# A new order of work for the attention of a sandwich layer, and its last chunk's rest at steps 24 and 25

## The chip, the cores and the metric

The kernel runs on one core of a Trainium2 chip. The metric is the device time of one launch in microseconds (us). The engines are TensorE (PE; its weight loads are shown apart as PEld), VectorE (DVE), ScalarE (ACT), GpSimd (POOL) and SyncE (SP), which here issues most of the DMAs. PE's clock has two levels, 1.2 and 2.4 GHz; a granted clock of 1.00 in the profile is the upper one.

## The reference

Input x is 4 x 2048 x 256 in float32. Biases, all of them drawn with a spread of 0.1, are left out of this sketch.

```
n   = layernorm(x)
q,k,v = n@wq, n@wk, n@wv                      # 16 heads of 16
s   = q @ k.T / 4, causal                     # 2048 x 2048 for each of 64 (batch, head) pairs
x   = x + layernorm(softmax(s) @ v @ wo)
n   = layernorm(x)
e   = the two best of 8 experts, by token 0 of each batch entry (n[:,0] @ Wr)
x   = x + layernorm(mean over both of gelu(n@W1[e]) @ W2[e])
```

## The kernel before

**Stage a** (to about 206 us) normalises x in 16 chunks of 512 tokens, multiplies out q, k and v and writes them to DRAM. q and k are written as three bf16 parts whose sum is the float32 value: ACT casts the high part (L1122), POOL subtracts it, ACT casts the middle part (`middle`, L972, 128 x 2048), DVE subtracts that for the low part (`low`, L976), and SP stores all three. For the last of the 16 chunks the middle, the low part and the store do not fit in stage a: they are handed to stage b as `rest_of_a`.

**Stage b** (about 206 to 1690 us) is the attention. It takes four heads at a time: `it` 0 to 7 and `g` 0 or 1 give 16 such groups. A group's 2048 queries are four chunks `c` of 512, and chunk c has 4(c+1) key tiles of 128. One (group, chunk, key tile) is a **key step** `j`; there are 640, 80 for each `it`, 40 for each group. A key step costs:

- scores, PE L1382: for each of four heads two products (64 rows of the array, then 33 rows), up to 512 columns, into the four banks of `b_psS`. Heads 0 and 2 use the lower 64 rows of the array (half 0), heads 1 and 3 the upper 64 rows (half 1).
- two exponentials, ACT L1339, each of two heads (128 x 1024 at full width), into `b_prob`, which holds four steps
- on the diagonal a causal mask on POOL, L1309
- values, PE L1399: four products of 128 rows x 32 columns of the array with float32 operands, all heads side by side, into `b_psO`. The trace shows 8 matmuls for one key step.
- at the end of a chunk a copy of `b_psO` (ACT L1349) and its store.

The exponent needs each row's greatest score beforehand, to subtract it. So PE computes the scores of a later chunk once more, roughly, into `b_ring` (L618, with L616 for the causal part of a diagonal block), and DVE takes their maximum from there (L628). The ring has three banks. There are 2336 such maximum jobs, each in one half of the array; 54 of them are done in stage a. When all jobs of a chunk are done, DVE reduces once more and transposes (L634, L644), SP stores the result and loads it again as a row of `g_qT` (L651, L655), and only then can the chunk's scores start.

DVE has three more duties in stage b. Once for each `it` from 1 on, at its step 20, it takes the reciprocals of the row sums of the `it` before (L236, `INVERT_AT`). Once, it takes the `low` of the last chunk of stage a. And at the end it runs `front`, the output projection and first layer norms of the first batch entry, which PE mixes with the last key steps.

**What sets the order.** PE, DVE, ACT and SP each walk the same list, `ORDER`, which `read_orders` makes of the strings in `ORDERS`. Each sign is one piece of work:

```
"0" "1"   the next score product of half 0 or 1 (4 of each half per key step)
"a" "b"   the next maximum job of half 0 or 1
"v"       the value product of the next key step
"p" "q" "r" "y" "l"   pieces of front: projection, two square roots, transposes, expert scores
```

The engines run each other's work free only through semaphores: a maximum job waits until DVE has emptied the bank three jobs back; the first score product of a pair of heads waits for the exponential of the same pair one key step back; a value product waits for both exponentials of its step. The strings were drawn up by a program outside the kernel; no cost model is in the kernel.

Where the rest is placed is read in the same walk. In ACT's loop, with `last` true for the last of the score products that an exponential waits for:

```
if last:
    exponentials(j, s)
if last and (j, s) == (REST_MIDDLE_AT, 1):
    rest_of_a.scalar(act)          # the cast, L972
```

and in DVE's loop `if last and (j, s) == (REST_LOW_AT, 1): rest_of_a.vector(v)` (L976, which first waits for the cast), and for the reciprocals `if last and s == 1 and at == INVERT_AT and it > 0: chunks.invert_sums(v, it - 1)`.

**Stage c** (from 1690 us) multiplies out the experts and the rest of the projections, chunk by chunk. It is the same code before and after.

## Time and profile before

| | |
|---|---|
| median of 3 runs | 1991.49 us |
| lowest, highest | 1989.31, 1994.93 us |
| the profiled execution's own time | 1991.74 us |
| its span in the trace | 1990.0 us |
| instructions | 39435 |

The profile counts an engine as busy while an instruction is in it. Two matmuls in the two halves of the array overlap, and the share counts their union, so a PE that is busy 98% of the time may still have one half idle. "Idle before" is the time in which an engine did nothing ahead of the instruction named, with the engine that ended the wait. In the timeline, instructions of one kind that follow each other stand in one row, with their count behind an x.

### The profile page before, as it was taken

The numbers are of one execution on the slowest core, as the hardware profiler recorded it, in microseconds if no ns is written. First come the engines' busy times: TensorE is split into PE (matmuls) and PEld (weight loads), VectorE is DVE, ScalarE is ACT, GpSimd is POOL, SyncE is SP. The second block draws the span as 40 slices with busy tenths as digits, with TensorE's granted clock in tenths as the row PEclk, the third lists the DMA queues.
The fourth block names the chain that finished last, engine by engine and source line by source line (L and its number), as shares of the span: only waits on it lengthen the run. The fifth ranks groups of instructions, "written<-read, shape, count | busy, mean of one in ns | idle before, by whom it ended". The sixth has DMA issues, their size and how long they took to land. (4 is left out here: it accounts for less than half of the span.)

```text
span 1990.0 us, 39435 instructions
## 1 busy us (share of the span) xinstructions
PE 1950.9 (98%) x15684; PEld 854.6 (43%) x15684; DVE 1784.6 (90%) x3574; ACT 1365.3 (69%) x1655; POOL 295.6 (15%) x358
## 2 busy tenths in 40 slices
PE   9999999999999999999999999999999998999998
PEld 6655333333333333333333333333333343667665
DVE  7876999999999999999999999999999985799984
ACT  5766757777777777777777777777777767333432
POOL 4333101011111111010111111110101211322100
PEclk9999999999999999999999999999999999999999
DMA  6877606040404124250504041232506213344321
GB/s 180 255 220 209 136 11 123 16 93 9 92 23 85 44 55 68 35 88 11 93 9 92 16 91 42 58 61 42 92 7 136 82 38 119 85 127 124 96 69 43
DMA packets 151706, 162.93 MB, mean 82 GB/s; under 512 B 58466, under 2 KB 124386, under 8 KB 151522
## 3 DMA queue, kind: packets, MB, share of 16 engines
q1 hardware_dynamic: 146658, 151.98, 32.7%
q0 software_dynamic: 4864, 8.44, 1.9%
q8 instruction: 123, 2.02, 0.4%
q14 instruction: 61, 0.50, 0.1%
HBM read 100.03 MB, written 60.29 MB: 81 GB/s over the span
## 5 line engine op out<-in xcount | busy, mean ns | idle before, releaser
L628 DVE TENSOR_REDUCE b_pmax<-b_ring 128x1 f32<-128x512 f32 (+4 forms) x2282 | 1329.0, 647 | 62.3 <-PE b_ring L618 51.1
L1339 ACT ACTIVATE b_prob<-b_psS 128x1024 f32<-128x1024 f32 (+3 forms) x1280 | 1084.8, 895 | 359.3 <-PE b_psS L1382 353.9
L1382 PE MATMUL b_psS<-g_qT,g_kT 33*128 33x512 bf16 (+7 forms) x5120 | 832.8, 348 | 9.8 <-ACT b_prob L1339 7.7
L618 PE MATMUL b_ring<-g_kT,g_qT 64*128 64x512 bf16 (+3 forms) x2498 | 712.1, 348 | 3.9 <-DVE b_pmax L628 2.1
L1399 PE MATMUL b_psO<-b_prob,g_v 128*32 128x512 f32 (+3 forms) x5120 | 595.5, 540 | 0.4 <-ACT b_outT L1349 0.3
L1382 PEld LDWEIGHTS b_psS<-g_qT,g_kT 64*128 64x128 bf16 (+1 forms) x5120 | 295.6, 94 | 462.7 <-ACT b_prob L1339 349.4
L1309 POOL TENSOR_SCALAR_AFFINE_SELECT b_prob<-b_prob 128x512 f32<-128x512 f32 x256 | 163.4, 638 | 1296.6 <-ACT b_prob L1339 1296.3
L618 PEld LDWEIGHTS b_ring<-g_kT,g_qT 64*128 64x128 bf16 x2498 | 220.5, 94 | 251.4 <-DVE b_pmax L628 177.7
L616 PE MATMUL b_ring<-later,query_of 64*128 64x128 bf16 x988 | 190.6, 219 | 2.0 <-DVE b_pmax L628 1.5
L1399 PEld LDWEIGHTS b_psO<-b_prob,g_v 128*32 128x32 f32 x5120 | 103.2, 108 | 168.0 <-issue 133.5
L1753 PE MATMUL c_psH<-c_yT,c_w1e 128*128 128x512 f32 x256 | 116.7, 604 | 10.4 <-ACT c_hT L1674 7.5
L1166 PE MATMUL a_psQK<-c_cc,a_w 128*128 128x512 f32 x256 | 115.8, 599 | 1.2 <-ACT c_cc L1086 1.2
L1766 PE MATMUL c_psO<-c_w2e,c_hT 128*128 128x256 f32 x512 | 113.4, 380 | 0.0
L616 PEld LDWEIGHTS b_ring<-later,query_of 64*128 64x128 bf16 x988 | 87.6, 94 | 54.9 <-DVE b_pmax L628 26.9
L1766 PEld LDWEIGHTS c_psO<-c_w2e,c_hT 128*128 128x128 f32 x512 | 97.0, 190 | 18.7 <-issue 6.2
L1674 ACT ACTIVATE c_hT<-c_psH,c_b1e 128x512 f32<-128x512 f32 x64 | 43.1, 686 | 53.8 <-PE c_psH L1753 53.7
L1753 PEld LDWEIGHTS c_psH<-c_yT,c_w1e 128*128 128x128 f32 x256 | 47.9, 192 | 69.8 <-issue 52.3
L1166 PEld LDWEIGHTS a_psQK<-c_cc,a_w 128*128 128x128 f32 x256 | 47.2, 190 | 54.6 <-issue 53.8
L1180 PE MATMUL a_psV<-a_w,c_cc 128*128 128x256 f32 x256 | 58.8, 383 | 0.0
L99 ACT ACTIVATE c_ln_x_std<-c_ln_x_var,eps 128x4 f32<-128x4 f32 x12 | 3.6, 297 | 76.1 <-DVE c_ln_x_var L95 76.1
L628 DVE TENSOR_REDUCE b_pmax<-a_ring 128x1 f32<-128x512 f32 (+4 forms) x54 | 31.1, 617 | 26.3 <-PE a_ring L618 26.2
L976 DVE TENSOR_TENSOR a_parts<-c_inv,a_parts 128x2048 bf16<-128x2048 f32 x16 | 36.7, 2292 | 19.8 <-ACT a_parts L972 19.8
(162 smaller groups left out, 1055.9 us busy)
## 6 DMA issues: line engine op xcount, KB each, us to landing
qk_parts<-a_parts SPq DMA_DIRECT2D x64, 384.0 KB, 4.5
g_qT<-qk_parts SPq DMA_DIRECT2D x184, 128.0 KB, 4.5
g_kT<-qk_parts SPq DMA_DIRECT2D x184, 128.0 KB, 5.0
out_sums<-b_outT SPq DMA_DIRECT2D x64, 256.0 KB, 2.9
v_ones<-a_v SPq DMA_DIRECT2D x16, 544.0 KB, 5.8
g_v<-v_ones SPq DMA_DIRECT2D x32, 272.0 KB, 4.9
a_x<-in_L_attn_x SPq DMA_DIRECT2D x16, 512.0 KB, 4.9
c_x<-in_L_attn_x SPq DMA_DIRECT2D x15, 512.0 KB, 5.0
```

The lines of the kernel that those rows point to most:

```text
L616: self.nc.tensor.matmul(to[:, w - P:w], consts.query_of[half:half + HALF, :], consts.later[half:half + HALF, :], start=True, stop=False, s ...
L618: ins_ = self.nc.tensor.matmul(to, groups.qT[own, g, h // 2, 0, t * P:(t + 1) * P], groups.kT[own, g, h // 2, 0, pc * CH:pc * CH + w], sta ...
L628: self.nc.vector.tensor_reduce(pmax[:, c % 2].rearrange("p (h t) n -> p h t n", t=TT)[:, heads[0]:heads[-1] + 1:2, qt, pc], bank[:, 0:k * ...
L1166: ins_ = nc.tensor.matmul(psQK[:, i % 2], w[:, t, k, m * P:(m + 1) * P], xT[:, n % 2, k], start=(k == 0), stop=(k == KD - 1))
L1180: ins_ = nc.tensor.matmul(psV[:, t], xT[:, n % 2, k, t * P:(t + 1) * P], w[:, 2, k], start=(k == 0), stop=(k == KD - 1))
L1309: nc.gpsimd.affine_select(out=tile, in_=tile, compare_op=ALU.is_ge, fill=0.0, base=0, pattern=[[0, HG], [1, P]], channel_multiplier=-1).th ...
L1339: nc.scalar.activation(prob[:, j % PBUF, 2 * s:2 * s + 2, off:CH], psS[:, 2 * s:2 * s + 2, off:CH], ACT.Exp).then_inc(exp_done, 1)
L1382: ins_ = nc.tensor.matmul(psS[:, 2 * s + p, off:CH], kT[own, g, s, ab, kt * P:(kt + 1) * P], qT[own, g, s, ab, c * CH + off:(c + 1) * CH], ...
L1399: ins_ = nc.tensor.matmul(psO[h * VW:(h + 1) * VW, off:CH], vS[:, g, kt, h * VC:h * VC + VW], prob[:, j % PBUF, h, off:CH], start=(kt == 0 ...
L1674: nc.scalar.activation(hT[:, e, m], psH[:, i % 2], ACT.Gelu, bias=experts[b % 2].b1[:, e, m:m + 1]).then_inc(gelu_done, 1)
L1753: ins_ = nc.tensor.matmul(psH[:, i % 2], experts[b % 2].w1[:, e, k, m * P:(m + 1) * P], yT[:, k, c], start=(k == 0), stop=(k == KD - 1))
L1766: ins_ = nc.tensor.matmul(psO[:, t], hT[:, e, m, t * P:(t + 1) * P], experts[b % 2].w2[:, e, m], start=(i == 0), stop=(i == 2 * KD - 1))
```

## The change

Three things change, all in numbers and strings.

```diff
-REST_MIDDLE_AT = 26
-REST_LOW_AT = 30
+REST_MIDDLE_AT = 24
+REST_LOW_AT = 25
 REST_STORED_AT = 34
...
 ORDERS = (
-    "a101a1010b0ab1010aa0101b1010av1a110bb0001v01ab010101b0101bv0b011a101aav0b0b011bbvb0101a1010bav1a1aa1010b"
+    "a1010b0a1b01a1010a0101ab0vab010101a1v0101b0101bb01010101avba1010bv0b011a101ab0vb0101aa1010bvb0101a1010ba"
...
```

The strings are new from the first sign to the last. They hold the same signs: 2560 each of "0" and "1", 1141 each of "a" and "b", 640 "v", 15 of the front. The program that draws them up now counts three more things: the reciprocals on DVE, the rest of the last chunk on ACT and DVE, and ScalarE's idle time. Nothing is computed otherwise.

**The rest.** On ACT, in stage b of the kernel before; the names are those of the rows above (`b_prob` exponentials, `b_outT` the copy out):

```order
L1339 ACTIVATE b_prob<-b_psS 128x2x128 x2
L1349 COPY b_outT<-b_psO 128x512
L1339 ACTIVATE b_prob<-b_psS 128x1024 x6
L972 CAST a_parts<-c_inv 128x4x512
L1339 ACTIVATE b_prob<-b_psS 128x1024 x20
```

The same place after the change:

```order
L1339 ACTIVATE b_prob<-b_psS 128x2x128 x2
L1349 COPY b_outT<-b_psO 128x512
L1339 ACTIVATE b_prob<-b_psS 128x1024 x2
L972 CAST a_parts<-c_inv 128x4x512
L1339 ACTIVATE b_prob<-b_psS 128x1024 x24
```

The cast moves ahead of four exponentials: it now follows the first pair of this chunk instead of the third. On DVE, around `low`, before:

```order
L628 TENSOR_REDUCE b_pmax<-b_ring 128x1 x5
L628 TENSOR_REDUCE b_pmax<-b_ring 128x2
L628 TENSOR_REDUCE b_pmax<-b_ring 128x1 x13
L976 TENSOR_TENSOR a_parts<-c_inv,a_parts 128x4x512
L628 TENSOR_REDUCE b_pmax<-b_ring 128x1 x2
```

and after:

```order
L634 TENSOR_REDUCE b_nmax<-b_pmax 128x16
L644 STREAM_TRANSPOSE b_nmT<-b_nmax 128x32
L628 TENSOR_REDUCE b_pmax<-b_ring 128x1 x3
L628 TENSOR_REDUCE b_pmax<-b_ring 128x2
L628 TENSOR_REDUCE b_pmax<-b_ring 128x1
L628 TENSOR_REDUCE b_pmax<-b_ring 128x2
L628 TENSOR_REDUCE b_pmax<-b_ring 128x1
L976 TENSOR_TENSOR a_parts<-c_inv,a_parts 128x4x512
L628 TENSOR_REDUCE b_pmax<-b_ring 128x1
```

`low` now comes seven reductions of jobs after the end of a chunk (L634, L644: group 1's first chunk) instead of far behind it. In the strings, the signs that follow the point of `low` are `10b0bv1ab01010b01a` before and `b0101a0101v101010b` after.

**A reciprocal.** On DVE, around the first of the seven reciprocals of stage b (the one at key step 100), before:

```order
L634 TENSOR_REDUCE b_nmax<-b_pmax 128x16
L644 STREAM_TRANSPOSE b_nmT<-b_nmax 128x32
L236 RECIPROCAL b_pair_sums<-b_pair_sums 128x128
L628 TENSOR_REDUCE b_pmax<-b_ring 128x2
L628 TENSOR_REDUCE b_pmax<-b_ring 128x1 x6
```

and after:

```order
L644 STREAM_TRANSPOSE b_nmT<-b_nmax 128x32
L628 TENSOR_REDUCE b_pmax<-b_ring 128x2
L628 TENSOR_REDUCE b_pmax<-b_ring 128x1 x3
L628 TENSOR_REDUCE b_pmax<-b_ring 128x2
L628 TENSOR_REDUCE b_pmax<-b_ring 128x1 x2
L236 RECIPROCAL b_pair_sums<-b_pair_sums 128x128
L628 TENSOR_REDUCE b_pmax<-b_ring 128x1 x5
```

The reciprocal no longer follows a chunk's end directly. What PE does between the jobs changes more than DVE's own order: the signs behind the reciprocal's point are `bbb1010v1aab001010ba1` before and `vba10101a100v1a110b0a` after, so three maximum jobs come at once before, and a value product, two jobs and five score products after.

**An ordinary stretch.** On PE, from one value product (L1399) to the next, behind the value product of key step 414, before:

```order
L1399 MATMUL b_psO<-b_prob,g_v 32x512 x4
L1382 MATMUL b_psS<-g_qT,g_kT 128x512
L618 MATMUL b_ring<-g_kT,g_qT 128x512 x2
L1382 MATMUL b_psS<-g_qT,g_kT 128x512 x7
L618 MATMUL b_ring<-g_kT,g_qT 128x512
L616 MATMUL b_ring<-later,query_of 128x128
L618 MATMUL b_ring<-g_kT,g_qT 128x512
```

and after:

```order
L1399 MATMUL b_psO<-b_prob,g_v 32x512 x4
L618 MATMUL b_ring<-g_kT,g_qT 128x512
L1382 MATMUL b_psS<-g_qT,g_kT 128x512 x4
L618 MATMUL b_ring<-g_kT,g_qT 128x512 x2
L1382 MATMUL b_psS<-g_qT,g_kT 128x512 x4
L618 MATMUL b_ring<-g_kT,g_qT 128x512
```

Both hold eight score products and four maximum jobs. After the change the two halves take turns, one maximum job of each half ahead of four score products and again behind them (the form `b0101ab0101a`); 27 stretches of the new order read exactly so, and 7 of the old.

## Rows read from the trace of the kernel before

**Rows 1.** The page's first part: span, busy time of each engine.
```profile
span 1990.0 us, 39435 instructions
PE 1950.9 (98%) x15684; PEld 854.6 (43%) x15684; DVE 1784.6 (90%) x3574; ACT 1365.3 (69%) x1655; POOL 295.6 (15%) x358
```

**Rows 2.** Busy time by stretch: stretch, length, then per engine; granted clock, DMA share, GB/s.
```profile
206.00:262.00 56.00, 55.41 (x496) 19.28 (x494) 55.79 (x98) 39.47 (x48) 7.84 (x12) 1.00 0.47 84
262.00:300.00 38.00, 34.07 (x280) 12.46 (x276) 34.17 (x63) 22.79 (x25) 1.24 (x2) 0.91 0.08 27
300.00:1630.00 1330.00, 1323.15 (x12618) 485.96 (x12613) 1267.57 (x2255) 1015.54 (x1231) 159.04 (x240) 1.00 0.30 59
1630.00:1690.00 60.00, 56.10 (x436) 22.61 (x428) 34.48 (x116) 42.34 (x52) 6.04 (x8) 1.00 0.35 115
```

**Rows 3.** PE's timeline, 801 to 808: start, length, instruction, count.
```profile
803.68 1.06 PE L1399 MATMUL b_psO<-b_prob,g_v 128*32 128x512 f32 x8
804.67 0.39 PE L1382 MATMUL b_psS<-g_qT,g_kT 64*128 64x512 bf16 x1
804.68 0.39 PE L618 MATMUL b_ring<-g_kT,g_qT 64*128 64x512 bf16 x1
804.90 0.60 PE L1382 MATMUL b_psS<-g_qT,g_kT 33*128 33x512 bf16 x3
805.12 0.38 PE L618 MATMUL b_ring<-g_kT,g_qT 64*128 64x512 bf16 x1
806.17 1.06 PE L1399 MATMUL b_psO<-b_prob,g_v 128*32 128x512 f32 x8
```

**Rows 4.** PE's timeline, two value products in one, and a stretch at 969 us.
```profile
1263.36 1.92 PE L1399 MATMUL b_psO<-b_prob,g_v 128*32 128x512 f32 x16
1265.21 0.61 PE L1382 MATMUL b_psS<-g_qT,g_kT 64*128 64x512 bf16 x4
...
969.48 1.06 PE L1399 MATMUL b_psO<-b_prob,g_v 128*32 128x512 f32 x8
971.97 0.64 PE L1399 MATMUL b_psO<-b_prob,g_v 128*32 128x512 f32 x4
```

**Rows 5.** Timeline at the first reciprocal: DVE, PE, and PE's weight loads.
```profile
449.55 0.91 DVE L236 RECIPROCAL b_pair_sums<-b_pair_sums 128x128 f32<-128x128 f32 x1
...
449.96 1.06 PE L1399 MATMUL b_psO<-b_prob,g_v 128*32 128x512 f32 x8
453.02 1.06 PE L1399 MATMUL b_psO<-b_prob,g_v 128*32 128x512 f32 x8
...
451.98 0.09 PEld L616 LDWEIGHTS b_ring<-later,query_of 64*128 64x128 bf16 x1 [0.28 <-DVE b_pmax L628]
```

**Rows 6.** Timeline, 261 to 295: DVE, ACT and PE around the rest.
```profile
261.88 0.22 DVE L634 TENSOR_REDUCE b_nmax<-b_pmax 128x16 bf16<-128x64 f32 x1
...
277.84 1.89 ACT L972 CAST a_parts<-c_inv 128x2048 bf16<-128x2048 f32 x1
...
289.91 2.28 DVE L976 TENSOR_TENSOR a_parts<-c_inv,a_parts 128x2048 bf16<-128x2048 f32 x1
...
268.30 0.60 PE L1382 MATMUL b_psS<-g_qT,g_kT 64*128 64x512 bf16 x1
280.71 0.39 PE L1382 MATMUL b_psS<-g_qT,g_kT 64*128 64x512 bf16 x2 [1.34 <-ACT b_prob L1339]
292.86 0.39 PE L618 MATMUL b_ring<-g_kT,g_qT 64*128 64x512 bf16 x1 [1.63 <-DVE b_pmax L628]
```

**Rows 7.** Granted clock in a stretch of its own, as Rows 2.
```profile
268.30:275.10 6.80, 6.78 (x37) 2.89 (x39) 5.52 (x11) 3.98 (x5) 0.00 (x0) 0.52 0.07 23
```

**Rows 8.** PE's timeline in the front, 1630 to 1680.
```profile
1630.47 3.72 PE L792 MATMUL b_ring<-wo,c_cc 128*128 128x256 f32 x16
...
1678.64 0.61 PE L1382 MATMUL b_psS<-g_qT,g_kT 64*128 64x512 bf16 x4 [0.68 <-ACT b_prob L1339]
```

**Rows 9.** DVE's timeline, six reductions in a row.
```profile
352.50 3.83 DVE L628 TENSOR_REDUCE b_pmax<-b_ring 128x1 f32<-128x512 f32 x6
```

**Rows 10.** DMA queue of SP, and DVE, at the end of a chunk, 1358 to 1361.
```profile
1358.94 0.57 SPq L651 DMA_DIRECT2D shifts<-b_nmT  x1
1360.91 1.17 SPq L655 DMA_DIRECT2D g_qT<-shifts  x2
...
1358.44 0.22 DVE L634 TENSOR_REDUCE b_nmax<-b_pmax 128x16 bf16<-128x64 f32 x1
```

More of the change, by code:

```diff
@@ new lines @@
+    "10b0101abva110b0a1vb0010101abva110110b00av01010b101a10b01av101ab0va1a0101010abva1010b0101abvb010101a10ba"
+    "va10101a10b0bvb01010b01a1ava1010b0101abvb0101a1010bavab01a101a1v0b1a10ba00ab0va11010b0a1v0b0001111bb0101"
+    "010b1ava1010ba0101a1010av1a100b1a10b0v0b101aa1010bv0b0101a101abv0b1a101a10b0va1010ba1010bva1010b011a0bva"
+    "1010ba1010bva1010ba1010bv0b0b011a101abvb0101a1010bava1010b0101abvba10101a1vb00b001a1v10100b011bb01010b01"
+    "1ava110b0b0101v0ba101v",
+    "0ba1010101va11100010bb0101avb0101ab0101avvb0101ab0101av0b1a10b010ba1va1010b0101abva110b0a1vb0010101abvb0"
@@ new lines @@
+    "01a1010ba1010bvvb0101a10b01av0b011a101a0bva1010b0101abva1010b0101abvb0101a1010bav1a100ba1010bv10101aa1a0"
+    "b0a100b1ab0101abv0b01a11010bava11010b001v0101ba1010a1010101ab0v1a100b10b01ava1010bb010a1v1a100bb0101ava1"
+    "010ba1010bvb0101a101a0bva1010b0101abvb0101ab0v1a10b01a10bva1010ba1010bbvb0101a101a0bva1010b0101abvb0101a"
+    "1010bavb0101a1010bav0b0101ab0va11010ba1v1010ba1010v0b011a1010bava110b0v",
+    "101ab01010bv0101010ba1v1010b0101ab0101av01a10bv1a100b01a10bva1010ba1010bva1010b0101abva1010b0b011avb0010"
@@ new lines @@
+    "010b0101b0101a1010bva1010bv0b1a1010a1b0v1a100bb010a1vb0101a1010bavb0101a1010bavb0101a10b01av0b01010bv1aa"
+    "1a101a0bvbab010101a10bv0b011ab010a1va110b00101v1010ba1010b1010100ba1va1010ba1010aa1010av1a10b0101a0bva10"
+    "1010ba10bv0b1a101a10b0vb0101ab0101ava1010b011a0bva1010b01a10bva1010b0101abv0b0b011a10a1bvb0101ab0101ava1"
+    "010b01a10bvb0101ab0va110101ab0va110101abv0b00101abv0b0011011ab0101av0b01a1v",
+    "0b01a10101bv1010ba1010vb00011101ab0101bvb0101b010b1avb0101aa1010bvb0101ab0101avb0101a10b01ava1100b0101ab"
@@ new lines @@
+    "a11v10101a100a1010bavva1010b01b0a1va1010b0101abvb0101a10b01ava1010b0101abvb0101a1010bava1010b0101aav0b1a"
+    "010b1aab01a1010bv0b011a1a10b0v1a10b010b01vb0010a1110vab01010101a01a10aa1010bv1a1001a10b0v1a1a0b01010bava"
+    "1010b0101abv0b1a10101ab0va1010b010ba1va1010b0101bavb0101a1010bava1010b0101abvb0101ab0101ava1010b0101abva"
+    "1010b01a10bvb0101ab0va1101ab010vab0101a11v0b0a11b00v1010b0101a10b01av0101abv",
+    "010ba10101bv10101ab010v0101a1010b0101bava1010a10ab01va01010b101abva1010b01a10bvb0101a10b01ava110b0a1vb00"
@@ new lines @@
+    "a11v0101a1010ba1010bvva1010b01a10bva1010b0101abvb0101a10b01ava10101ab010bva1010b0b01a1va10101a1a00av0b1a"
+    "1a010b1ab0bv0b011a0b01a1v0b01a10101avb0010101b1bb10100101b1010a1010bav1ab010010ba1v0b01a1v0b1a1010b01av0"
+    "ba10b01011av1a0b01a1010bv1a10b010a1b0vb0101a1a100bvb0101a1010bavb0101a10b01ava10101a10b0bvb0101a10b01avb"
+    "0101ab0101ava1010ba1vb001a110b0vb00101ab0v1a1b00a11v10101a100b0101abv0101abv",
+    "1a10b01010av01010b0a11v0101a1010b0b011av101a0bvb0101ab0101avb0101ab0101avb0101ab0101ava1010b01a10bvb0010"
@@ new lines @@
+    "0v10101ab010b0101avvb0101a1010bavb0101a10b01av0b011a1a100bva1010ba1010bvb0101ab0101avb0101a1010bav1aa101"
+    "a10b0b0v010b1ab100b1bb0101bb0011avb0010101a1av01010b011bb01010b01a1va1010b0b011ava1010ba1010bvb0101a101a"
+    "b0vb0101ab0101av1a0b010b01a1va1010b0101abvb0101a1010abv0b01a101a10bvb0101ab0101ava1010b010ba1vb0101a1010"
+    "bavb0101a1010bavab0101a1vb0010b0a11vb001001a11v1010b0101a0b01a1va110b0a1010v0b0a11v",
+    "010b001a11bv0b0011011ab0101va1010ba1010bv1a10b0v1a10b0a1010bva1010b101ab0va1010b0101aava110101ab00vb0010"
@@ new lines @@
+    "1010ba1010bvvb01a10b0101avb0101a10b01ava10101a10b0bvb01010b01a1ava1010b01a10bvb0101a101ab0vab0101a0b101a"
+    "bv1a100bb0101abv0ba1101010bava110b00101va11010100aa0101a1010bvb0101abva1010b0101bav1a1a1010a0b0avb0101a1"
+    "0b01av0b01a10b01a1vb0101a1010bav0b011a0b01a1vba10101010bavb0101a1010bav0ba1010b01a1vb0101a10b01avb0101a1"
+    "00ba1vb01010abva110b001a1vb00101ab011v0b0a111100a01010b01a1vb001a1v",
+    "0b011a1010bva1b001a1100v10100ba101010b1avvb0101a1010bavb0101ab0101avb0101a0b01a1vb0101a1010bavb001a1b010"
```

122 lines of the change are left out of this document (43 added, 79 removed).

## The prediction

> **What bounds the kernel now.** I read the page's first part, then the busy time by stretch, then the timeline. The reader is to see first that PE is busy 98% of a span of 1990.0 us [rows 1], and in the body of the attention, 300 to 1630 us, 1323.15 of 1330 us; DVE stands at 1267.57 there, ACT at 1015.54 [rows 2]. PE is the bound, but its busy share hides an idle half of the array. So the length has to be read between value products, which need the whole array.
>
> An ordinary stretch: value products start at 803.68 and 806.17, 2.49 us apart. The next product starts 0.99 us after the first; products in the two halves start together (804.67 and 804.68), and each half takes a new 512-column product about every 0.22 us, 512 columns at 2.4 GHz [rows 3]. This stretch has 3072 columns in each half, 1.28 us, so a full-width value product costs 1.21 us. Two value products with nothing between take 1.92 us as a row and the next score product comes 1.85 us after the first: 0.88 + 0.97 [rows 4]. So each passage from half-array products to a value product and back costs 0.32 us.
>
> I walked the old order with two rules from these rows: a product starts when its half is free and not before the one ahead of it; value products cost as above, shorter ones in proportion to their columns. A check where the halves are balanced (2560 columns each) but two jobs of one half follow each other: columns alone give 2.28 us, the walk 2.49, and the products stand at 969.48 and 971.97, 2.49 apart [rows 4]. From the first value product to the last of the 640 the walk gives 1443.8 us, the trace 1479.6. The rest, 35.8 us, I place so:
> - front's projections and transposes on PE, not in the walk: four blocks of 3.55 us (3.72 with the overlapping tail [rows 8]) and two of 0.8 for transposes, 15.8 us. They stay.
> - the first 40 stretches: 9.8 us. DVE is busy 55.79 of 56 us up to 262 and is the bound there [rows 2]; group 0 needs all maxima of its last chunk before key step 24. They are done at 261.88 and the scores start at 268.30 only [rows 6], then run at a granted clock of 0.52, the lower level, to 275.1 [rows 7]. The cast holds PE 1.34 us, `low` 1.63 us [rows 6].
> - the seven reciprocals, 4.5 us in the eight stretches around each. At the first, value products stand 3.06 us apart, where columns give 2.28 (2560 in each half), and PE waits for DVE with 0.28 us at 451.98 [rows 5].
> - waits for ACT in the tail, such as 0.68 us at 1678.64 [rows 8]: 4.5 us. The rest, 1.2 us, is scattered.
>
> **The change part by part.** It adds and removes no instruction; everything is order.
>
> Columns. In each stretch between value products the fuller half counts. Summed over all stretches that is 1,808,896 columns before and 1,798,400 after: 10,496 fewer at 2400 per us, **-4.4 us**. Where one half gets two products in a row, the other waits: the walk's surplus over the fuller half falls from 10.6 to 5.8 us, **-4.8 us** (stretches that lose over 0.08 us in this way: 49, now 26). Value products that follow another directly fall from 23 to 13: ten more passages at 0.32 us, **+3.2 us**. Together -6.0 us. This term rests on counts, and the walk met the quiet middle (stretches 41 to 600) within 5.1 us of 1275, of which 4.5 are the reciprocals; I give it 1 us either way. No wait hides it: PE is the engine at work.
>
> A rule of the Trainium skill bears on the +3.2: "TensorEngine Tiling (Array Packing)", Key Properties, says that changing the tiling mode drains the engine. The rows agree in kind, with 0.32 us for a passage there and back; the page gives no size. It is the part of this change that goes the wrong way.
>
> Reciprocals. Each takes 0.91 us on DVE [rows 5]. A reduction of 512 columns takes about 0.62 us in a row of six (3.83 us [rows 9]), and four in 2.49 us is near DVE's limit, so a reciprocal sets the ring back by more than one bank. In the old order the fourth job behind the reciprocal's point comes 2.0 to 2.3 us later in six of seven cases (columns and value products counted), in the new one 3.3 to 3.9 us in five of seven. DVE needs 0.91 + 0.62 for the first bank. I take **-3.3 us** of the 4.5; bounds 0 (PE's surplus of work there was bought with a wait elsewhere) and -4.5.
>
> The rest. The cast (1.89 us) now comes between the exponentials of step 24 and those of 25, `low` (2.28 us [rows 6]) one step later. Behind ACT's cast, which no longer has an idle stretch ahead of it, stand the exponentials of step 25 and the ones of 26; PE waits there for the bank of step 26, about 3.1 us of its own work later, against 1.89 + 0.92 + the score's own way: a wait of 0 to 1 us where it was 1.34. Behind `low`, DVE may wait for the cast up to 1.5 us, and with `low` is away 3.8 us; the fourth job behind it comes after 4.7 us in the new order, 2.2 us in the old, so the 1.63 us go. But DVE's summed work is ahead of PE's by more: at the stretch of `low` the summed reductions less PE's walk stand at 7.9 us after and 7.1 before, which takes up to 0.8 us back. The queue of SP is not touched: the store stays at step 34. I take **-1.5 us** for the first 40 stretches beside the columns; bounds -6 (all waits and the slow clock gone) and +2.5.
>
> The clock. For 6.8 us PE ran at the lower level, behind 6.3 us in which it waited for DVE again and again [rows 6, 7]. The new order is just as dense in maxima there (16 jobs between the end of the last chunk's maxima and step 24's first score, 15 before), so I expect the fall to stay. It is half of 6.8, 3.4 us, that hangs on it. "TensorE: Matmul & The Clock Gate", Terms, prices it alike, throttled time times the missing share of pulses; by that page's rule a fall avoided gives 3.4 us more and a second fall takes as much.
>
> The tail. From the first projection on, the walk is equal (40.1 us each). The new order puts 4, not 8, score products behind the second projection and eight between the transposes where none stood: **-0.4 us**; bounds -3 and +2.
>
> The sum: -6.0 - 3.3 - 1.5 - 0.4 = -11.2 us, from the profiled execution's 1991.74 us 1980.5 us. The profiled execution lies 0.25 us above the median of the runs; I leave that in the rounding and predict **1980.5 us**.
>
> **The rivals.**
> - The gain is the column term and more: the clock does not fall, and all waits at the reciprocals and the rest go. -6.0 - 4.5 - 6 - 2 = -18.5: about 1973 us. For it: one job fewer stands ahead of step 24's first score (108, from 109), and PE's walk to it is 1 us shorter. Against: DVE is the bound in that place in both orders.
> - It is taken back: no change. The columns saved lie where PE had to wait for a bank of the ring or of the scores anyway, so a fuller half costs nothing there. For it: in the body ACT and DVE both leave PE little room, and the stretches that lose most by the walk are often those around a chunk's end, dense in jobs. Half of -9.2 and half of the reciprocals gone, +3.2 kept: 1988 to 1990 us. Against: the old walk meets the body without such waits; a stretch of 2560 columns with two jobs in one half lasts exactly as walked [rows 4].
> - DVE falls behind, which makes it slower. With four full-width jobs a stretch lasts 2.49 us by PE [rows 3], and DVE needs 4 x 0.62 = 2.48 [rows 9]. There are 222 such stretches between the 41st and the 600th in the new order (234 in the old, where they last 2.50 on the mean). If a regular order takes from DVE the pauses in which it caught up, and each is paced by DVE at 2.60, that is +22 us, less 11: about 2003 us. It decides from 0.08 us per stretch on: 222 x 0.08 = 17 us is what turns -11 into +6. Against: DVE idles 62 us of the body's 1330 [rows 2], and the old order had runs of 12 such stretches, the new one of 10 at most.
> - The maxima arrive late. From the last reduction of a chunk (1358.44) to the first load of the shifts' row 2.47 us pass [rows 10]; with the second load and a landing as long as the store's 1.97 us it is 5.6 us, and DVE may run three banks, 1.9 us, behind. The walk's distance from a last chunk's last job to its first score is 7.4 us at the least in both orders (the first group apart). At 8.5 us for the way one or two groups would wait 1 us: +1, inside the range.
>
> **How the numbers follow.** Forecast (1976 to 1985) 0.58; the larger gain 0.13; taken back, 1986 to 1991, 0.19; DVE behind, slower, 0.08; late maxima 0.02. From no change a measurement of this kernel tells about 0.3%, 6 us. The forecast and the larger gain lie beyond it but for the forecast's upper edge: faster 0.72, within 0.3% 0.20, slower 0.08. The range runs from the larger gain to the edge of no change, 1973 to 1989.5 us.
>
> **What would show it.** In the changed profile: 640 value products whose first and last lie some 1468 us apart, not 1479.6; stage c unchanged at about 300 us; DVE's busy time unchanged and its idle time smaller by about 10 us; no wait of PE for DVE at `low`; the cast's wait under 1.1 us; at the reciprocals stretches within 0.3 us of their columns. It is wrong if the first 40 stretches take over 109 us (106.6 before), if stretches with four full-width jobs last over 2.55 us, or if a chunk's first score products stand behind an idle PE.

## The result and the profile after

| | before | after |
|---|---|---|
| median | 1991.38 us (4 runs) | 1978.20 us (4 runs) |
| lowest, highest | 1989.31, 1994.93 us | 1973.95, 1982.12 us |
| the profiled execution's own time | 1991.74 us | 1982.12 us |

The ratio of the runs is 0.9932, with a 95% interval from 0.9906 to 0.9957: the change makes the kernel about 13 us faster. The forecast was 1980.5 us. It is close, but two of its steps were wrong in opposite directions, as the rest of this text shows.

The page's first part of the changed kernel, which answers to [rows 1]:

```profile
span 1980.4 us, 39435 instructions
PE 1940.9 (98%) x15684; PEld 852.9 (43%) x15684; DVE 1782.0 (90%) x3574; ACT 1363.6 (69%) x1655; POOL 294.7 (15%) x358
```

DVE is busy 2.6 us less and ACT 1.7 us less, PE 10 us less in a span 9.6 us shorter. The shares tell nothing: the gain has to be read from stretch to stretch, as before.

The busy time by stretch of the changed kernel, in the order of [rows 2]: PE, PEld, DVE, ACT, POOL, granted clock, DMA share, GB/s.

```profile
206.00:262.00 56.00, 55.28 (x488) 19.59 (x488) 55.60 (x95) 39.23 (x48) 8.77 (x12) 1.00 0.44 86
262.00:300.00 38.00, 36.98 (x319) 13.94 (x317) 36.10 (x68) 26.03 (x28) 0.63 (x1) 0.96 0.20 62
300.00:1528.00 1228.00, 1225.31 (x11811) 452.15 (x11807) 1184.87 (x2115) 945.98 (x1150) 140.83 (x222) 1.00 0.31 59
1528.00:1545.00 17.00, 10.51 (x78) 4.17 (x79) 7.34 (x14) 5.90 (x9) 1.27 (x2) 0.60 0.53 145
1545.00:1620.00 75.00, 74.55 (x695) 26.09 (x691) 71.86 (x125) 58.79 (x71) 16.92 (x16) 1.00 0.09 29
1620.00:1680.00 60.00, 56.00 (x428) 22.55 (x420) 33.92 (x116) 42.60 (x52) 4.90 (x8) 1.00 0.35 115
```

Up to 262 us little has changed: PE is busy 55.28 us and DVE 55.60, where they were 55.41 and 55.79. From 262 to 300 PE is busy 36.98 us where it was 34.07. From 300 to 1528 us PE is busy 99.8% of the time. Then comes one hole: in the 17 us from 1528 on it works 10.51 us, and its clock is granted at 0.60 there.

By value products, counted as in the prediction (a stretch runs from one value product's start to the next one's; all times from the two timelines):

| stretches | before, us | after, us | change |
|---|---|---|---|
| 1 to 40 | 106.58 | 101.72 | -4.9 |
| 41 to 600, but 582 to 584 | 1268.55 | 1253.29 | -15.3 |
| 582 to 584 | 6.48 | 16.76 | +10.3 |
| 601 to 639 | 97.96 | 98.51 | +0.6 |
| first to last value product | 1479.6 | 1470.3 | -9.3 |

From the last value product to the end, which is stage c, it takes 300.1 us, 300.2 before. So the new order saves some 20 us in two places and loses 10.3 us in one.

**The loss.** SP's queue in the changed kernel at that place (start, length, instruction). L249 and L250 are the loads of contexts and inverse sums for `front`; L651 and L655 store a chunk's maxima and load them again as a row of `g_qT`, here for the last chunk of the next to last group, whose scores begin with key step 584.

```profile
1511.10 0.64 SPq L249 DMA_DIRECT2D c_cc<-out_sums  x1
...
1521.07 2.10 SPq L250 DMA_DIRECT2D c_inv<-inverse_sums  x1
1523.21 1.00 SPq L651 DMA_DIRECT2D shifts<-b_nmT  x1
1533.25 1.20 SPq L655 DMA_DIRECT2D g_qT<-shifts  x2
```

The timeline of DVE and PE at the same place, changed kernel:

```profile
1520.95 0.22 DVE L634 TENSOR_REDUCE b_nmax<-b_pmax 128x16 bf16<-128x64 f32 x1
...
1528.97 0.38 PE L618 MATMUL b_ring<-g_kT,g_qT 64*128 64x512 bf16 x1
1535.84 1.03 PE L1382 MATMUL b_psS<-g_qT,g_kT 64*128 64x512 bf16 x4 [6.49 <-DMA g_qT<-shifts]
...
1537.33 1.02 DVE L628 TENSOR_REDUCE b_pmax<-b_ring 128x2 f32<-128x256 f32 x2 [7.25 <-PE b_ring L618]
```

DVE's last reduction for the maxima starts at 1520.95. The store L651 is issued at 1523.21, behind twelve loads of front, and the load L655, which waits for the store's landing, 10.0 us later. PE stands still for 6.49 us. Within this wait its clock falls to the lower of its two levels, and it stays there from 1531.2 to 1544.8 us, for 9.0 us of which PE works. From 1530 to 1545 us the granted clock is 0.54.

```profile
1530.00:1545.00 15.00, 9.16 (x62) 3.84 (x66) 5.41 (x10) 4.66 (x6) 0.35 (x1) 0.54 0.53 137
```

In the kernel before, DVE's last reduction started at 1539.16, the store followed 0.5 us later, and store and load stood 3.3 us apart:

```profile
1539.66 0.56 SPq L651 DMA_DIRECT2D shifts<-b_nmT  x1
1542.98 1.20 SPq L655 DMA_DIRECT2D g_qT<-shifts  x2
```

**The rest.** DVE, ACT and PE of the changed kernel around the cast and `low`, which answer to [rows 6]:

```profile
262.14 0.22 DVE L634 TENSOR_REDUCE b_nmax<-b_pmax 128x16 bf16<-128x64 f32 x1
...
272.10 1.89 ACT L972 CAST a_parts<-c_inv 128x2048 bf16<-128x2048 f32 x1
...
275.88 2.29 DVE L976 TENSOR_TENSOR a_parts<-c_inv,a_parts 128x2048 bf16<-128x2048 f32 x1
...
274.83 0.39 PE L618 MATMUL b_ring<-g_kT,g_qT 64*128 64x512 bf16 x1 [0.20 <-DVE b_pmax L628]
```

PE's waits of 1.34 us for the cast and 1.63 us for `low` are gone; the longest idle time of PE from 262 to 300 us is 0.21 us. The group's last maxima are as late as before (262.14, before 261.88), and the clock fell again, for 3.4 us where it was 6.8 [rows 7]:

```profile
268.30:271.70 3.40, 3.40 (x21) 1.93 (x22) 2.78 (x7) 2.03 (x3) 0.00 (x0) 0.51 0.00 0
```

**A reciprocal.** DVE in the changed kernel at the place of [rows 5]:

```profile
445.85 0.94 DVE L236 RECIPROCAL b_pair_sums<-b_pair_sums 128x128 f32<-128x128 f32 x1
446.70 1.69 DVE L628 TENSOR_REDUCE b_pmax<-b_ring 128x1 f32<-128x512 f32 x3
448.58 0.69 DVE L628 TENSOR_REDUCE b_pmax<-b_ring 128x1 f32<-128x512 f32 x1 [0.20 <-PE b_ring L618]
```

DVE has caught up after three reductions and waits for PE again. The seven places took 4.5 us over the walk before and 0.6 us less than the walk with the same order and no hole at 1528 (the first experiment).

### The profile page after: what moved, and what is told of

The parts are those of the page before. It is cut to its first block and busy times, and to the rows that moved or that the text cites. A ratio compares the mean times of both kernels' runs of the same rounds, so it can differ in the third digit from the quotient of the medians.

```text
span 1980.4 us, 39435 instructions
## 1 busy us (share of the span) xinstructions
PE 1940.9 (98%) x15684; PEld 852.9 (43%) x15684; DVE 1782.0 (90%) x3574; ACT 1363.6 (69%) x1655; POOL 294.7 (15%) x358
## 5 line engine op out<-in xcount | busy, mean ns | idle before, releaser
L628 DVE TENSOR_REDUCE b_pmax<-b_ring 128x1 f32<-128x512 f32 (+3 forms) x2282 | 1327.2, 647 | 54.0 <-PE b_ring L618 42.9
L1382 PE MATMUL b_psS<-g_qT,g_kT 64*128 64x512 bf16 (+7 forms) x5120 | 823.4, 348 | 13.0 <-DMA g_qT<-shifts 6.5
L618 PE MATMUL b_ring<-g_kT,g_qT 64*128 64x512 bf16 (+3 forms) x2498 | 727.3, 348 | 1.6 <-ACT a_v L1097 0.9
L1399 PE MATMUL b_psO<-b_prob,g_v 128*32 128x512 f32 (+3 forms) x5120 | 598.3, 541 | 0.7 <-POOL b_prob L1309 0.3
L618 PEld LDWEIGHTS b_ring<-g_kT,g_qT 64*128 64x128 bf16 x2498 | 225.6, 94 | 399.9 <-DVE b_pmax L628 338.0
L1399 PEld LDWEIGHTS b_psO<-b_prob,g_v 128*32 128x32 f32 x5120 | 102.3, 108 | 164.6 <-issue 130.8
L1753 PE MATMUL c_psH<-c_yT,c_w1e 128*128 128x512 f32 x256 | 116.8, 605 | 10.3 <-ACT c_hT L1674 7.4
```

The lines of the kernel that those rows point to most:

```text
L618: ins_ = self.nc.tensor.matmul(to, groups.qT[own, g, h // 2, 0, t * P:(t + 1) * P], groups.kT[own, g, h // 2, 0, pc * CH:pc * CH + w], sta ...
L628: self.nc.vector.tensor_reduce(pmax[:, c % 2].rearrange("p (h t) n -> p h t n", t=TT)[:, heads[0]:heads[-1] + 1:2, qt, pc], bank[:, 0:k * ...
L1382: ins_ = nc.tensor.matmul(psS[:, 2 * s + p, off:CH], kT[own, g, s, ab, kt * P:(kt + 1) * P], qT[own, g, s, ab, c * CH + off:(c + 1) * CH], ...
L1399: ins_ = nc.tensor.matmul(psO[h * VW:(h + 1) * VW, off:CH], vS[:, g, kt, h * VC:h * VC + VW], prob[:, j % PBUF, h, off:CH], start=(kt == 0 ...
L1753: ins_ = nc.tensor.matmul(psH[:, i % 2], experts[b % 2].w1[:, e, k, m * P:(m + 1) * P], yT[:, k, c], start=(k == 0), stop=(k == KD - 1))
```

## The experiments

Times are medians; "before" was run beside each group: 1990.54, 1991.02 and 1989.92 us. "Body" is the stretches 41 to 600. Each profile tells of one execution. Two orders that agree up to some point agree in the traces there to a few hundredths of a microsecond, the granted clock and the DMAs apart, so differences within the body are read from the traces, where the medians can't tell them. In experiments 5 to 10 and 12 front's loads are at steps 20 to 23 as in experiment 1 (`FRONT_LOAD_AT = 20`); the diffs leave that line out. For the new order experiment 1 is therefore the kernel to compare with. For the old one this line was not tried by itself; its stretches 582 to 584, where the loads stood, last 6.28 us with it and 6.48 without.

### 1. Front's loads behind the maxima's row

```diff
-FRONT_LOAD_AT = 16
+FRONT_LOAD_AT = 20
```

> The changed kernel with front's 12 loads of context and inverse sums (FRONT_LOAD_AT) at steps 20 to 23 of the last pair of groups instead of 16 to 19, so behind the store and load of the shifts' row of the last chunk of group (7, 0). Theory A (the 10.7 us that stretches 582 to 584 take over their work in the changed kernel's profile come from SP's queue: L655 issued 10.0 us behind L651, with 12 loads ahead of it): L655 comes 3 to 4 us behind L651, PE waits there under 0.5 us, the three stretches lie within 1 us of the walk, and the time is 8 to 11 us under that profile's 1982.1: 1971 to 1974, about 5 to 7 under the changed kernel's median of 1978.2, since its runs differ in how long that wait is. Rival B (the maxima themselves come too late in the new order, whatever stands in the queue): the wait stays at 4 us or more, and the time at 1977 to 1982. Rival C (the loads come later and hold up front or the next shifts' row instead): stage c or the last 24 stretches grow by over 3 us and the time is again about 1977.

Measured: 1972.42 us, ratio to before 0.9915 (0.9901 to 0.9928). SP's queue in this kernel:

```profile
1521.67 0.56 SPq L651 DMA_DIRECT2D shifts<-b_nmT  x1
1523.63 1.17 SPq L655 DMA_DIRECT2D g_qT<-shifts  x2
```

The load is issued 2.0 us behind the store, PE has no wait there, and the stretches 582 to 584 last 6.06 us instead of 16.76. That is 10.7 us, and theory A holds. Of the 10.7 us, 6.5 are the wait; the other 4.2 go with the lower clock, at which PE did 9.0 us of work. The profiled execution is 10.7 us shorter too (1971.45 against 1982.12), but that the two figures are alike is chance: stage c, whose code and order are the same, is 2.9 us shorter in it, and all stretches but these three are 2.9 us longer in their sum, 1.1 of it in stretches 585 to 600. The whole body is 9.6 us shorter. The medians lie 5.8 us apart, and the profiled execution of the changed kernel is the slowest of its four, so the others probably lose less there. Rival C falls: stage c and the last 23 stretches are not longer in their sum (297.2 and 62.2 us, against 300.1 and 60.6). What differs in them goes for the greater part with the clock, which fell for 3.4 us at 1633 us here and not there, and at 1931 us there and not here:

```profile
1633.08:1636.48 3.40, 3.40 (x20) 0.52 (x15) 3.26 (x15) 1.94 (x2) 0.64 (x1) 0.50 0.33 122
```

No kernel that leaves nothing out was faster. The interval of this one overlaps that of the changed kernel a little; the two were not timed side by side.

### 2 and 3. The constants without the strings, and the strings without the constants

```diff
-REST_MIDDLE_AT = 26
-REST_LOW_AT = 30
+REST_MIDDLE_AT = 24
+REST_LOW_AT = 25
```

on the old strings alone:

> The kernel before with the rest of the last chunk at steps 24 and 25 (REST_MIDDLE_AT, REST_LOW_AT), the order unchanged: the constants without the strings. Theory A (the order carries the change, the place of the rest does little or harm by itself, since the old order has few jobs to spare for it there): first 40 stretches 106 to 110 us (106.6 before), the time 1990 to 1995. Rival B (the earlier rest is what shortened the first 40 stretches by 4.9 us): they take 101 to 103 us and the time is 1986 to 1988. In both, the stretches from the 41st on are as before.

and the reverse on the new strings:

> The changed kernel with the rest back at steps 26 and 30, the new strings kept: the strings without the constants. Theory A (the strings carry it): first 40 stretches 101 to 105 us (101.7 after the change), a cast's wait and a low's wait of 1 to 2 us each come back at most, and the time is 1978 to 1982, 0 to 3 us over the changed kernel. Rival B (the constants carry the first stretches' 4.9 us): 105 to 108 us there and the time 1982 to 1985. In both the stretches from the 41st on are as after the change, its long wait before stretch 584 among them, as far as it comes in a run.

Measured: 1990.75 us (ratio 1.0002, 0.9993 to 1.0011) and 1981.79 us (0.9960, 0.9946 to 0.9973). The stretches 1 to 40 last 103.6 and 104.1 us. How often the clock falls near 268 us differs from execution to execution, with the same instructions up to there, so I compare executions with the same fall as far as there are any. Stretches 21 to 30:

| | rest at 26 and 30 | rest at 24 and 25 |
|---|---|---|
| old strings | 34.3 us without a fall (experiment 11), 36.35 with 6.8 us of it | 33.4 us with 3.4 us of it |
| new strings | 32.8 us without | 29.6 us without (experiments 6, 7, 8, 12), 30.4 with 3.4 us |

A fall of 3.4 us costs 0.8 us here, one of 6.8 us 2.1 us; PE waits for DVE in part of it anyway. In the old strings the earlier rest is worth some 1.7 us, in the new ones 3.2 us. Each alone gives less than both together. In the third kernel PE waits at `low` again, 1.67 us at 290.76, as it did before [rows 6]. Theory A of experiment 2 is right in the time and wrong in the trace: its own profiled execution is 2.5 us shorter than before's, the medians are the same. The mean clock of its eleven runs is mostly 0.995, that of before beside them mostly 0.998; where they lose it no profile shows, and that stays open.

The third kernel's hole is shorter than the changed kernel's, with the same order at that place: L655 comes 8.0 us behind L651, and PE waits

```profile
1534.40 0.61 PE L1382 MATMUL b_psS<-g_qT,g_kT 64*128 64x512 bf16 x4 [2.55 <-DMA g_qT<-shifts]
```

2.55 us instead of 6.49. How long twelve loads hold the row up is not fixed.

### 4. The new strings up to the 181st value product, the old ones behind

```diff
 ORDERS = (
     "a1010b0a1b01a1010a0101ab0vab010101a1v0101b...      # new, 2337 signs
-    ...
+    ...                                                # old, the rest
```

> The new strings up to the 181st value product, the old ones behind it (both orders have done the same work at that point); rest at 24 and 25. If the gain is spread over the order as it was measured in the two profiles (8.4 us up to that point, 9.1 from there to stretch 575, then a loss of 7.9 at the wait before stretch 584), this kernel gains the 8.4 alone: 1982 to 1984, with the waits around the second to seventh reciprocal as before (0.5, 0.5, 0.7, 1.0, 1.0, 0.3 us) and none before stretch 584. Rival: the part behind depends on how far DVE is when it starts, and what the first part gains is given back in the second: then 1988 to 1991.

Measured: 1984.73 us (0.9968, 0.9956 to 0.9980), 0.7 us above the theory's range. The stretches 1 to 180 last 417.7 us, as after the change (before 426.2), 181 to 575 897.6 against 896.2 before and 887.0 after. The gain stays where the order is new; 1.4 us are given back behind the seam. Of the 8.5 us that the new order saves up to the seam 4.9 are in the first 40 stretches, and what it saves behind them is spread over the body.

### 5 and 6. Reciprocals of one column

```diff
-        self.nc.vector.reciprocal(self.pair_sums[:, :], self.pair_sums[:, :]).then_inc(self.sums_inv, 1)
+        self.nc.vector.reciprocal(self.pair_sums[:, 0:1], self.pair_sums[:, 0:1]).then_inc(self.sums_inv, 1)
```

> The order before, with the reciprocals of the row sums cut to one column of 128 (L236; the other sums are left uninverted, so this part of the computation is left out), and front's loads at step 20 to 23. Theory A (each reciprocal's 0.91 us of DVE costs PE 0.3 to 1.0 us in the old order, 4.5 us in seven places): the stretches around the seven fall from 4.5 us over the walk to between -1 and 0.5, and the time lies 4 to 6 us under before: 1985 to 1987. Rival B (the ring's waits there come from the jobs' own order, three jobs at once, not from the reciprocal): 2 to 4 us over the walk stay, and the time is 1988 to 1990.

> The order after the change with front's loads at steps 20 to 23, and the reciprocals cut to one column in the same way. Theory A (the new order hides them): nothing or less than 1 us to gain in the seven places (-0.6 us over the walk in their sum with them, between -1.5 and -0.5 without), time 1971 to 1973 as with them. Rival B (they only cost elsewhere now: DVE is 0.9 us later and the wait comes more than four stretches behind): the stretches from 41 to 600 shorten by 2 to 4 us and the time is 1968 to 1970.

Measured: 1987.40 us (0.9982, 0.9971 to 0.9992) and 1971.62 us (0.9900, 0.9878 to 0.9922). In the old order the body falls from 1275.0 to 1271.9 us, 3.1 us; the seven places keep 1.25 us over the walk. In the new order it goes from 1260.50 to 1260.35. So the new order hides the reciprocals wholly, theory A. For the old order the result lies between the two theories, nearer to A: A had at most 0.5 us left in the seven places and 1987 us at most, B 2 us and 1988 at the least. Of the 5.1 us that the change saves around them, some 3 are the reciprocals and 2 the jobs beside them. And with no reciprocals in either, 11.6 us between the two orders are left.

### 7. Products of the halves in pairs instead of in turn

```diff
-va1010b0101abv
+va1100b0011abv
```

in 92 stretches of this and three like forms.

> The order after the change with front's loads at steps 20 to 23, and in 92 stretches of the regular kind (such as b0101ab0101a) the score products of the halves no longer in turn but in pairs (b0011ab0011a): the same columns in each half, the same jobs at the same places. Theory A (two products of one half in a row leave the other half idle, for as long as the walk says): the 92 stretches last 0.104 us longer on the mean, 9.6 us in all, and the time is 1981 to 1983 against 1972.4. Rival B (PE waits in those stretches for a bank of the ring or of the scores anyway, so that columns saved or lost there count half or nothing): 0 to 5 us more, 1972.5 to 1977.

Measured: 1973.08 us (0.9905, 0.9882 to 0.9928), nothing. The 92 stretches last 226.69 us, 226.63 with the products in turn; the walk had 9.6 us more. PE's timeline of one such stretch in this kernel:

```profile
470.70 1.06 PE L1397 MATMUL b_psO<-b_prob,g_v 128*32 128x512 f32 x8
471.70 0.39 PE L616 MATMUL b_ring<-g_kT,g_qT 64*128 64x512 bf16 x1
471.70 0.82 PE L1380 MATMUL b_psS<-g_qT,g_kT 64*128 64x512 bf16 x4
...
473.19 0.64 PE L1397 MATMUL b_psO<-b_prob,g_v 128*32 128x512 f32 x4
```

2.49 us, where the walk gives 2.70. So both theories fall. Rival B would let the pairs cost a half; they cost nothing. By the walk all of the 9.6 us lie in 52 of the 92 stretches (the form above and its mirror image, 0.18 us each); in the other 40 pairs cost nothing by the walk either. Those 52 last 2.477 us in turn and 2.478 in pairs. DVE's pace can't hide the difference: in 26 of them the walk gives 2.70 us, 2.62 with the value product at the lower price of experiment 10, and they last 2.497 us on the mean. The rule that a product never starts before the one ahead of it, on which the walk stood, does not hold: one of the free half overtakes the one that waits for its own half. The order of work in this stretch is `a1100b0011ab`. Behind `b` come the 64-row and the 33-row product of half 0, then those of half 1. In order, the 64-row product of half 1 would start with or behind the 33-row one of half 0. PE's rows up to 472.37 show two 64-row products and no 33-row one behind the job at 472.15:

```profile
472.15 0.38 PE L616 MATMUL b_ring<-g_kT,g_qT 64*128 64x512 bf16 x1
472.36 0.38 PE L1380 MATMUL b_psS<-g_qT,g_kT 64*128 64x512 bf16 x2
```

Their 33-row products both start at 472.58. The prediction's check of the rule was the stretch from 969.48 to 971.97 [rows 4], and it was no check. The weight loads of the kernel before, which the prediction did not take in there, show what held its last job up:

```profile
971.64 0.09 PEld L618 LDWEIGHTS b_ring<-g_kT,g_qT 64*128 64x128 bf16 x1 [0.19 <-DVE b_pmax L628]
```

It waited for DVE. Experiment 9 takes that wait away.

### 8. Value products merged in the new order

```diff
-va1101010b0v10b0010ba11v
+va1101010b010b0010ba11vv
```

at 18 places.

> The order after the change with front's loads at steps 20 to 23, and 18 value products of the body moved back to stand directly ahead of the next one, each where the two stretches together hold at most five maximum jobs. It takes 18 passages between value products and half-array products away; columns and order of the halves stay. Theory A (a passage costs 0.32 us there and back, and where jobs are few nothing takes it back): 5.8 us less, 1966 to 1968 against 1972.4. Rival B (the jobs and scores that now follow each other without a value product between make PE wait for DVE's banks or ACT's exponentials): the merged stretches last as long as before or longer, 1971 to 1976.

Measured: 1992.81 us (1.0007, 0.9995 to 1.0020); the body is 21.8 us longer, 1.2 us for each merge. PE's timeline from one value product to the merged pair in this kernel:

```profile
879.17 1.06 PE L1397 MATMUL b_psO<-b_prob,g_v 128*32 128x512 f32 x8
...
881.79 0.28 PE L1380 MATMUL b_psS<-g_qT,g_kT 64*128 64x256 bf16 x2 [0.67 <-ACT b_prob L1337]
...
882.82 1.71 PE L1397 MATMUL b_psO<-b_prob,g_v 128*32 128x512 f32 x16
```

The two stretches took 3.74 us apart. Merged, their score products take 3.65 us up to the first value product and the pair adds 0.88, 4.53 us together. PE stands idle for 0.67 us in the middle and waits for an exponential: 16 score products fill the banks of two key steps one after the other, the second only when ACT has emptied the first, and the value product in whose time ACT did that is gone. The row is of one merge; that the others cost for the same reason is argued from it. Rival B, and harder than it was put: the time lies 17 us over its upper edge.

### 9 and 10. Maxima over half the columns

```diff
-            bank[:, 0:k * w].rearrange("p (k w) -> p k w", k=k), AX.X, ALU.max).then_inc(self.ring_free, 1)
+            bank[:, 0:k * w].rearrange("p (k w) -> p k w", k=k)[:, :, 0:w // 2], AX.X, ALU.max).then_inc(self.ring_free, 1)
```

> The order before (front's loads at steps 20 to 23), with each of DVE's maximum reductions (L628) over the first half of its columns alone; the other half of the columns is left out of the maxima. PE's and ACT's work and order are as before. It stands beside the next kernel, which is the same with the new order. DVE, busy 1267.57 of 1330 us in the body, is out of PE's way here. Theory A of the prediction (PE's columns, counted per half and in order of the products, set the length, and DVE only adds waits at a few places): the stretches from 41 to 600 fall from 1275.0 to about the walk, 1265 to 1270 us. Rival B (DVE paces the stretches with four jobs: 4 x 0.62 = 2.49 us, what PE's columns give as well): they fall further, to 1255 to 1262, and value products with pairs of one half between them, such as 969.48 to 971.97, stand 2.28 us apart as their columns say, not 2.49.

> The new order with front's loads at steps 20 to 23 and the halved reductions of the kernel beside it. Theory A (columns and in-order surplus make the new order shorter, 5.2 us by the walk between stretch 41 and 600): it stays 5 to 6 us shorter than the old order with halved reductions in these stretches, about 1260 there. Rival B (what the new order saves are waits for DVE; without them columns give 4.4 us less and ten passages 3.2 us more): the two differ there by 0 to 2 us.

Measured: 1964.30 us (0.9870, 0.9854 to 0.9885) for the old order, 1943.68 us (0.9762, 0.9747 to 0.9777) for the new. The body lasts 1252.4 and 1236.1 us. For the old order that is rival B, and below even its range. The stretch that the expectation names is the same one as from 969.48 to 971.97 in the kernel before:

```profile
952.39 1.07 PE L1399 MATMUL b_psO<-b_prob,g_v 128*32 128x512 f32 x8
...
954.61 0.64 PE L1399 MATMUL b_psO<-b_prob,g_v 128*32 128x512 f32 x4
```

It lasts 2.23 us, not 2.49. With the value product at 1.13 us (below) its columns give 2.20. The two jobs of one half in a row cost next to nothing there, so the walk's rule fails for maximum jobs in this stretch as well. The busy time from 300 to 1560 us in the new order with halved maxima (PE, PEld, DVE, ACT, POOL, clock):

```profile
300.00:1560.00 1260.00, 1256.84 (x12351) 460.34 (x12347) 802.87 (x2210) 988.28 (x1203) 152.46 (x234) 1.00 0.31 61
```

DVE is at 64% and no longer in anybody's way. Two things follow. First, both orders are faster by 23 and 24 us in the body: PE waited that long for DVE in them. An ordinary stretch of the new order with whole maxima, value products and the last job's weight load (two views):

```profile
471.57 1.06 PE L1399 MATMUL b_psO<-b_prob,g_v 128*32 128x512 f32 x8
...
474.06 0.64 PE L1399 MATMUL b_psO<-b_prob,g_v 128*32 128x512 f32 x4
```

```profile
473.74 0.09 PEld L618 LDWEIGHTS b_ring<-g_kT,g_qT 64*128 64x128 bf16 x1 [0.19 <-DVE b_pmax L628]
```

and the same stretch with halved maxima:

```profile
465.77 1.07 PE L1399 MATMUL b_psO<-b_prob,g_v 128*32 128x512 f32 x8
...
468.17 0.64 PE L1399 MATMUL b_psO<-b_prob,g_v 128*32 128x512 f32 x4
```

2.49 us become 2.40. The value product and its passage cost 1.13 us, not the 1.21 that I read from 803.68 and 806.17 [rows 3]; 0.08 us of that was a wait for DVE. Second, the new order is 16.3 us shorter than the old one with DVE out of the way, against 14.5 with it (experiment 1 against before). Theory A said 5 to 6, rival B 0 to 2: both fall. What the new order saves is not a wait for DVE alone, and not the columns alone.

### 11 and 12. Value products taken apart

```diff
-000111a10ba1010vvba101010b01a
+000111av10ba1010vba101010b01a
```

at 20 places of the old order, and

```diff
-vb0101ab0101avvb0101ab0101av
+vb0101avb0101avb0101ab0101av
```

at 11 of the new.

> The order before, with 20 value products of the body that stood directly behind or ahead of another moved to the middle of the neighbouring stretch; all else as before. It adds 20 passages, as the change added ten net. Theory A of the prediction (a passage costs 0.32 us there and back): 6 to 7 us more, 1996 to 1998 against 1990.5. Rival B (a value product standing alone gives ACT and DVE time to empty banks in which PE otherwise waits, as the merged kernel lost 1.2 us per merge): 0 to 15 us less, 1976 to 1990.

> The new order with front's loads at steps 20 to 23, and the 11 value products of the body that still stand next to another moved to the middle of the stretch ahead. Theory A (0.32 us a passage): 3.5 us more than the 1972.4 without it, about 1976. Rival B (what a lone value product lets ACT and DVE catch up is worth more): 0 to 8 us less, 1964 to 1972.

Measured: 2003.23 us (1.0061, 1.0047 to 1.0074) and 1975.59 us (0.9934, 0.9920 to 0.9947). The body grows by 11.5 us for 20 passages and by 4.1 us for 11: 0.58 and 0.37 us each, where the walk had 0.35 and 0.32. No sign of rival B. For the new order theory A holds. For the old one its sign holds and its size doesn't: the time lies 5 us above its range. By the prices of experiment 10 a passage alone costs 0.25 us (1.13 less 0.88). What the experiments show above that are waits that it brings; for which engine is not shown.

## Where the time went, by the new account

With the price of experiment 10 each stretch of the body has a floor: the fuller half's columns, and 1.13 us for a full-width value product with its passage (less for narrower ones, 0.88 where another stands directly ahead). The rest is waiting, an estimate that rests on these two prices.

| body, us | before | new order (experiment 1) | change |
|---|---|---|---|
| floor | 1218.6 | 1217.2 | -1.5 |
| waits: seven reciprocals, eight stretches each | 10.4 | 4.5 | -5.9 |
| waits: 12 or more score products (51, 52 stretches) | 16.8 | 9.7 | -7.1 |
| waits: 8 to 11 score products and four or more jobs (282, 283) | 25.3 | 24.5 | -0.8 |
| waits: all others | 3.9 | 4.7 | +0.8 |
| sum | 1275.0 | 1260.5 | -14.5 |

The same table for the two kernels with halved maxima gives 15.6 and 7.7 us for the stretches of 12 or more score products. So it is there, where a chunk ends and jobs and narrow score products crowd, that the old order lost time, and it loses it with a fast DVE too. The prediction's surplus, wrong as a mechanism, still pointed at stretches that wait: 41 stretches of the old body and 16 of the new one have over 0.08 us of it, and their waits are 15.4 us before and 4.5 in experiment 1, 11.4 and 2.7 with halved maxima. The waits in these stretches are of three kinds, for ACT, for DVE and for the array's own half, which follow on one another; how much each has of the 7.1 us is not settled.

## Why the prediction was right, and where it was not

- **Columns, -6.0.** This is a step that failed: the size was off and one of its parts was no mechanism. The floor fell by 1.5 us in the body, columns and passages together. The surplus of the walk (-4.8 of the -6.0) rested on products starting in order; experiment 7 shows that score products don't, and the stretch of 2.23 us in experiment 9 that jobs needn't. The price of 1.21 us for a value product held a wait for DVE of 0.08 us, in stretches with four jobs. What came in its place, -7.1 us in the long stretches, was not foreseen: the prediction names stretches "around a chunk's end, dense in jobs" only as a place where savings would be taken back.
- **Passages, +3.2.** Right in sign, and near in size: 0.37 us each by experiment 12, 0.58 by experiment 11, and 0.25 by the prices of experiment 10, which leave waits out. The Trainium skill ("TensorEngine Tiling (Array Packing)", Key Properties: a change of the tiling mode drains the engine) agrees with it in sign. But putting more value products in a row is no remedy: 18 merges cost 21.8 us (experiment 8).
- **Reciprocals, -3.3.** They gave -5.1 by the walk's account, just outside the bound of -4.5: jobs around them changed as well. Their own part is some 3 us (experiment 5).
- **The first 40 stretches, -1.5 and the walk's 1.1.** They gave -4.9, inside the bounds; about 1.3 us of it is a clock fall half as long. The prediction priced the fall at half its length, 3.4 us for 6.8; it costs 2.1 us here, since PE waits for DVE in part of it anyway. The fall stayed, as expected, but it is no property of the order: with the same instructions it came in experiments 1 and 4 and not in 3, 6, 7, 8 and 12.
- **The tail, -0.4.** +0.6 in stretches 601 to 639, inside the bounds; with the clock fall at 1633 us (experiment 1) it is +2.1.
- **The maxima arrive late.** This rival was given a chance of 0.02 and a price of 1 us. It came true with 10.7 us in the profiled execution, and so did a sign that the prediction had named for being wrong, a chunk's first score products behind an idle PE. The step that failed took the way of the row from [rows 10] as a constant, 5.6 us, and compared it with a distance counted on PE. What was not counted is the place in SP's queue. In both orders front's loads go out in this stretch, eight ahead of the row before and twelve now, since the end of the chunk's maxima moved against the steps at which SP loads. The prediction looked at SP's queue only for the rest's store ("The queue of SP is not touched").
- **DVE falls behind.** It did not: the 222 stretches last 2.499 us, 2.503 in the old order (they are those with four jobs and eight score products; not all of the jobs are full-width). But they were near DVE's pace already: with halved maxima they last 2.446 us in the old order and 2.439 in the new. "PE is the bound" was wrong there; PE and DVE need the same time within 0.1 us, and the 98% of PE's share holds the wait.

In the sum: forecast -11.2 us, the profiled execution gave -9.6. Without the late row the order gives -20.3 us from profile to profile (1971.45 us), of which 3.0 are stage c and not the order's, and -18.1 in the medians. So the gain was sized 6 to 9 us too small, and a loss of 10.7 us in the profiled execution was missed. That the two cancel is luck. In the medians the loss is 5.8 us, and 1978.2 lies a little under the forecast.

## What to carry to other kernels

A model of an engine that meets its total within 0.4% can still be wrong in its rules: test each rule on a row that nothing else can explain, and read the weight loads' waits there before a duration is taken for a price. (A weight load's idle time is not PE's: read it for what ended the wait, and PE's own row for how long.) Where an order of work moves against fixed points (here the steps at which one queue sends its loads), list for each small transfer that someone waits for what now stands ahead of it on its queue. Two engines that need the same time per stretch look like one that is busy 98%; halve the other one's work once to see it.

## What the runs showed of the hardware

- A small store followed by a load that waits for it took 2.0 us from issue to issue with front's loads behind it (experiments 1, 5 to 10 and 12), 3.3, 3.7, 5.5 and 6.0 us with eight loads ahead (before, experiments 11, 4 and 2), and 8.0 and 10.0 us with twelve (experiment 3, the changed kernel).
- A product of one half of the array starts ahead of an earlier one of the other half that still waits for its own: 92 stretches with score products in pairs last as long as in turn, 226.69 and 226.63 us, where starting in order would have added 9.6 us. How far ahead a product can start was not tried.
- A wait of PE of 6.5 us came with 13.7 us at the lower clock level (1531.2 to 1544.8 us, changed kernel), 9.0 of them at work, which cost 4.2 us beside the wait. A wait of 2.55 us was followed by 3.4 us at that level (1536.0 to 1539.5 us, experiment 3) and 1.6 us of cost.
- The clock near 268 us fell for 0, 3.4, 6.8 or 10.2 us in executions whose instructions there are alike (new strings: 3.4 in experiments 1 and 4, 0 in 7; old strings: 6.8 before, 10.2 in experiment 5, 0 in experiment 11).
